# Four-layer block on one core: the token mix moved to VectorE, and token chunks 2 and 3 handled as one chunk of 1024 columns between the value stage and the step sizes

## The reference, cut to what matters

```
x = layernorm(x + attention(x))            # channel attention, 16 heads of 8
x = layernorm(x + ffn(x))                  # the change is in this layer and the next
x = layernorm(x + ssm(x))
x = layernorm(x + mlp(x))                  # 128 -> 512 -> 512 -> 512 -> 128

ffn:  x_prev = x shifted by one token (zero ahead of the first)
      xr = mu_r*x + (1-mu_r)*x_prev ;  xk = mu_k*x + (1-mu_k)*x_prev
      out = sigmoid(xr @ W_r) * (square(relu(xk @ W_k)) @ W_v)

ssm:  lifted = tanh(relu(x @ Wl1 + bl1) @ Wl2 + bl2)
      xt = relu(concat(x, lifted) @ Wf1 + bf1) @ Wf2 + bf2
      B = xt @ W2 + b2 ;  C = xt @ W3 + b3 ;  delta = softplus(xt @ W1 + b1)
      h = exp(-celu(delta*A)) * h0 + xt * delta * B       # 16 states, no recurrence over tokens
      out = sum over states of C * h
```

## Time and profile before

| what | us |
|---|---|
| median of 3 runs (lowest to highest) | 257.53 (257.16 to 259.03) |
| the profiled execution | 257.19 |
| its span, first to last instruction | 255.1 |
| busy of PE, DVE, ACT, POOL in the span | 230.5, 203.0, 185.4, 122.8 |

### The profile page before, as it was taken

One profiled execution on the slowest core, in us unless ns is written; L12 is line 12 of the kernel. 1 busy time (PEld: TensorE's weight loads), 2 busy tenths in 40 slices (PEclk: granted clock), 3 DMA queues, 4 the chain that ended last, 5 costly groups with the idle time before them and its releaser, 6 DMA issues.

```text
span 255.1 us, 2677 instructions
## 1 busy us (share of the span) xinstructions
PE 230.5 (90%) x871; PEld 151.4 (59%) x871; DVE 203.0 (80%) x328; ACT 185.4 (73%) x255; POOL 122.8 (48%) x96
## 2 busy tenths in 40 slices
PE   6898899999999867999686999999999899999981
PEld 6888557545433234545233556578888678888860
DVE  4996892698377799997999989980599997996454
ACT  4787799989898699979998986369943743643433
POOL 3410000000046998899999983473344578054220
PEclk9999999999999955999997999999999999999996
DMA  5960000000000000000000000000000000110002
GB/s 137 377 260 1 1 3 0 0 0 0 0 0 0 0 5 1 3 0 0 1 1 0 0 0 3 0 0 0 0 0 3 0 0 3 42 41 0 1 0 82
DMA packets 4847, 6.16 MB, mean 24 GB/s; under 512 B 384, under 2 KB 2656, under 8 KB 4832
## 3 DMA queue, kind: packets, MB, share of 16 engines
q1 hardware_dynamic: 4832, 5.97, 6.9%
HBM read 4.92 MB, written 1.05 MB: 23 GB/s over the span
## 4 chain that ended last, share of the span: by engine, by line
PE 47%; DVE 22%; ACT 11%; POOL 10%; issue 6%; DMA 2%; SPq 0%; ACTq 0%; POOLq 0%; DVEq 0%
PE ps L1419 8%; PE ps L1420 8%; PE ps L1309 6%; PE ps L217 3%; PE ps L219 3%; PE ps L218 3%; POOL bs L420 3%; PE ps L1207 3%; DVE tr L1060 2%; DMA bx<-in_x_dram 2%; PE ps L1285 2%; POOL tr_f L412 2%; DVE xr L1057 2%; DVE tr L1057 2%; POOL bxt L399 1%
## 5 line engine op out<-in xcount | busy, mean ns | idle before, releaser
L733 ACT ACTIVATE bs<-ps,vec 128x512 f32<-128x512 f32 x48 | 31.7, 690 | 37.3 <-PE ps L1420 34.9
L1285 PE MATMUL ps<-tr,h0sel 96*128 96x512 f32 x64 | 26.5, 530 | 10.8 <-DVE bx L967 3.8
L389 POOL CAST tr<-bs 96x512 fp32r<-96x512 f32 x4 | 2.4, 607 | 59.2 <-ACT bs L632 59.0
L1285 PEld LDWEIGHTS ps<-tr,h0sel 96*128 96x128 f32 x64 | 12.7, 215 | 24.1 <-issue 11.8
L1419 PE MATMUL ps<-xr,wf 128*128 128x512 f32 x64 | 25.4, 396 | 0.0
L1420 PE MATMUL ps<-xr,wf 128*128 128x512 f32 x64 | 25.3, 396 | 0.0
L462 POOL TENSOR_TENSOR xr<-bs,xr 128x512 fp32r<-128x512 f32 x12 | 16.1, 1347 | 14.0 <-DVE xr L1057 14.0
L462 POOL TENSOR_TENSOR tr<-bs,tr 128x512 fp32r<-128x512 f32 x8 | 10.9, 1361 | 22.3 <-DVE tr L1057 22.3
L462 POOL TENSOR_TENSOR x1r<-bs,x1r 128x512 fp32r<-128x512 f32 x12 | 13.5, 1128 | 9.5 <-DVE x1r L1057 9.5
L1057 DVE CAST tr<-bs 128x512 fp32r<-128x512 f32 x16 | 7.4, 488 | 13.3 <-ACT bs L733 13.3
L1309 PE MATMUL ps<-bx,centre 128*128 128x512 f32 x28 | 16.5, 726 | 0.0
(11 more groups left out here) (228 smaller groups left out, 678.4 us busy)
## 6 DMA issues: line engine op xcount, KB each, us to landing
wf_raw<-in_w_mlp_dram SPq DMA_DIRECT2D x2, 1024.0 KB, 8.6
bx<-in_x_dram SPq DMA_DIRECT2D x4, 256.0 KB, 5.3
out_dram<-bdl SPq DMA_DIRECT2D x4, 256.0 KB, 2.3
wf_raw<-in_w_mlp_dram SPq DMA_DIRECT2D x1, 768.0 KB, 12.5
bdl<-in_w_ssm_dram SPq DMA_DIRECT2D x1, 448.0 KB, 7.9
wa<-in_w_attn_dram SPq DMA_DIRECT2D x1, 256.0 KB, 2.7
w0raw<-in_w_ffn_dram SPq DMA_DIRECT2D x1, 192.0 KB, 7.3
h0T<-in_state_dram SPq DMA_DIRECT2D x1, 48.0 KB, 5.4
```

The source lines that it names most:

```text
L733: a.activation(hbuf[k][:, o, :], ring(mbank(i, stage, k, o)), ACT.Gelu if stage else ACT.Silu, scale=vec[:, s + o:s + o + 1]).then_inc(m_a ...
L1285: last = m.matmul(ps[:, 2 * j + k, :], h0sel[:, group_states(e)[j], :], tr[0:96, 0, cs(2 * (e // NG) + k)], start=True, stop=True)
```

## The change

1. The token mix leaves PE and its weights. DVE writes x straight into `x1_f32` (`first_input`), takes x - x_prev (`token_step`), and makes both mixes by one scalar_tensor_tensor each (`token_mix`). PE then needs one plain fp32 matmul for the key and one for the receptance of a chunk. `w0f`, `w0`, `mu1` and what made them go; the split of x goes.
2. Chunks 2 and 3 become one instruction of 1024 columns over two PSUM banks: on ACT from the key's Relu to `c_copy`, on DVE in `transformed`, `bounded`, `step_size`, `c_times_b`, `weighted`. The square of the second norm is merged for chunks 0 and 1 as well. `gate` and `second_input` stay single.
3. All four queues are reordered around it.

```diff
+            def first_input(c):
+                dve.wait_ge(y1_rs, c + 1)
+                v.tensor_tensor(shifted(0, c, 2), ps[:, 4 + c, :], bs2[:, cs(c)], ALU.mult).then_inc(x1_ok, 1)
+            def token_step(c):
+                dve.wait_ge(x1_ok, c + 1)
+                v.tensor_tensor(bx2[:, cs(c)], shifted(0, c, 2), shifted(0, c, 1), ALU.subtract).then_inc(step_ok, 1)
+            def token_mix(c, mu, dst):
+                dve.wait_ge(step_ok, c + 1)
+                v.scalar_tensor_tensor(dst, bx2[:, cs(c)], vec[:, mu:mu + 1], shifted(0, c, 1), ALU.mult,
+                                       ALU.add).then_inc(mixed, 1)
+            def mixes(c):
+                token_mix(c, MU_K, bx1[:, cs(c)])
+                token_mix(c, MU_R, shifted(1, c, 2))
```

```diff
             gate(0)
+            gate(1)
+            state_weights(11, 12)
+            gate(2)
+            gate(3)
+            state_weights(12, 14)
+            second_input(0)
+            second_input(1)
+            fill_low(5)
+            second_input(2)
             fill_low(6)
             fill_low(7)
...
             second_input(3)
...
             transformed(0)
             transformed(1)
+            fill_low(8)
             bounded(0)
+            fill_low(9)
             bounded(1)
+            state_weights(14, NS)
+            step_size(0)
             c_times_b(0)
-            step_size(0)
             step_size(1)
+            fill_low(10)
             c_times_b(1)
-            weighted(0)
             dve.wait_ge(a_ok, 2)
             dve.wait_ge(d_ps, 2)
-            state_v(0)
+            state_v(0, range(1))
+            weighted(0)
+            state_v(0, range(1, GN))
+            transformed(2, 2)
+            state_v(1)
             weighted(1)
-            transformed(2)
-            transformed(3)
-            state_v(1)
-            c_times_b(2)
-            c_times_b(3)
+            c_times_b(2, 2)
+            bounded(2, 2)
+            weighted(2, 2)
             dve.wait_ge(low_mm, 1)
             v.tensor_reduce(low_any[:, :], ps[:, FLAG_BANK, 0:NLOW], AX.X, ALU.add).then_inc(low_flag, 1)
-            bounded(2)
-            weighted(2)
-            weighted(3)
-            bounded(3)
             state_v(2)
             state_p(0)
+            step_size(2, 2)
             state_v(3)
-            step_size(2)
-            step_size(3)
             state_p(1)
```

ScalarE's new order (the second argument is the count of chunks):

```diff
             act.preload_act_table(ACT.Tanh)
+            receptance(0)
+            key_relu(0)
+            key_relu(1)
+            key_square(0)
+            receptance(1)
+            key_square(1)
             low_magnitude(0)
+            key_relu(2, 2)
+            key_square(2, 2)
+            receptance(2, 2)
+            square(y2_mm, y2_sq, 0, 2)
+            act.preload_act_table_set(LN_EXP)
+            rstd_of(y2_var, y2_ln, y2_rs, 0)
+            rstd_of(y2_var, y2_ln, y2_rs, 1)
+            square(y2_mm, y2_sq, 2, 2)
             fill_high(2 * FILL, 2 * FILL + 1)
...
             layer1(0)
+            rstd_of(y2_var, y2_ln, y2_rs, 2, 2)
             layer1(1)
             act.preload_act_table(ACT.Tanh)
             layer2(0)
+            layer2(1)
+            low_magnitude(1)
+            fill_high(2 * FILL + 1, 2 * FILL + 2)
+            layer1(2, 2)
+            fusion(0)
+            fusion(1)
             low_magnitude(2)
+            layer2(2, 2)
             act.preload_act_table_set(LN_EXP)
...
             log_exp(0)
+            fill_high(2 * FILL + 2, 2 * FILL + 3)
             log_ln(0)
             log_exp(1)
+            c_copy(0)
             log_ln(1)
             c_copy(1)
             act.wait_ge(a_ok, 2)
+            fusion(2, 2)
             state_t(0)
             state_t(1)
+            c_copy(2, 2)
+            low_magnitude(3)
             state_t(2)
             state_da(0)
             log_exp(2, 2)
+            log_ln(2, 2)
             state_t(3)
             state_da(1)
```

More of the change, by code:

```diff
@@ L422, in _ @@
             c_parts(0)
+            c_parts(1)
             pool.wait_ge(a_ok, 2)
@@ L557, in _ @@
                 rstd_of(y1_var, y1_ln, y1_rs, c)
[L559 to L566, removed]
-            def layer1(c):
-                act.wait_ge(l1_mm, c + 1)
-                a.activation(bs1[:, cs(c)], ps[:, 4 + c, :], ACT.Relu, bias=vec[:, BL1:BL1 + 1]).then_inc(l1_ok, 1)
@@ L573, in layer2, with receptance @@
-            def layer2(c):
-                act.wait_ge(l2_mm, c + 1)
-                a.activation(bs3[:, cs(c)], ps[:, c, :], ACT.Tanh, bias=vec[:, BL2:BL2 + 1]).then_inc(l2_ok, 1)
-            def fusion(c):
-                act.wait_ge(f1_mm, c + 1)
-                a.activation(bs1[:, cs(c)], ps[:, 4 + c, :], ACT.Relu, bias=vec[:, BF1:BF1 + 1]).then_inc(f1_ok, 1)
+            def receptance(c, count=1):
+                act.wait_ge(rec_mm, c + count)
+                act.wait_ge(y1_var, c + count)
+                a.activation(span(bs1, c, count), ps[:, c:c + count, :], ACT.Tanh, scale=0.5).then_inc(th_ok, count)
@@ new lines, in key_relu, with key_square, layer1 @@
+            def key_relu(c, count=1):
+                act.wait_ge(key_mm, c + count)
+                a.activation(span(bs2, c, count), ps[:, 4 + c:4 + c + count, :], ACT.Relu).then_inc(relu_ok, count)
+            def key_square(c, count=1):
+                s = slice(c * CH, (c + count) * CH)
+                act.wait_ge(relu_ok, c + count)
+                a.activation(bs3[:, s], bs2[:, s], ACT.Square).then_inc(k2_ok, count)
+            def layer1(c, count=1):
+                act.wait_ge(l1_mm, c + count)
+                a.activation(span(bs1, c, count), ps[:, 4 + c:4 + c + count, :], ACT.Relu,
+                             bias=vec[:, BL1:BL1 + 1]).then_inc(l1_ok, count)
@@ new lines, in layer2, with fusion @@
+            def layer2(c, count=1):
+                act.wait_ge(l2_mm, c + count)
+                a.activation(span(bs3, c, count), ps[:, c:c + count, :], ACT.Tanh,
+                             bias=vec[:, BL2:BL2 + 1]).then_inc(l2_ok, count)
+            def fusion(c, count=1):
+                act.wait_ge(f1_mm, c + count)
+                a.activation(span(bs1, c, count), ps[:, 4 + c:4 + c + count, :], ACT.Relu,
+                             bias=vec[:, BF1:BF1 + 1]).then_inc(f1_ok, count)
@@ L943, in c_times_b @@
-            def c_times_b(c):
-                dve.wait_ge(c_full, c + 1)
-                v.scalar_tensor_tensor(products[:, cs(c)], ps[96:128, c, :], vec[96:128, B23:B23 + 1],
-                                       bs3[0:32, cs(c)], ALU.add, ALU.mult).then_inc(bc_ok, 1)
-            def weighted(c):
-                dve.wait_ge(bc_mm, c + 1)
-                v.tensor_tensor(bxt[:, cs(c)], bxt[:, cs(c)], ps[:, c, :], ALU.mult).then_inc(w_ok, 1)
-            def state_v(e):
-                for j, n in enumerate(group_states(e)):
+            second_input(3)
@@ L956, in state_v @@
+            def state_v(e, group=range(GN)):
+                for j in group:
+                    n = group_states(e)[j]
                     if not v_on_pool(e, j):
```

223 lines of the change are left out of this document (96 added, 127 removed).

## The result

The changed kernel takes 261.33 us (median of 20 runs, 258.97 to 263.58); the kernel before, run beside it, takes 258.55 us (20 runs). The ratio is 1.0098, with a 95% interval of 1.0064 to 1.0133: slower by 2.5 us on 257.5. The two medians alone would give 1.0108; the ratio leaves out five of the 20 changed executions, those more than 1.5% above the fastest, all at a mean granted clock of 0.945 or less. The forecast was 258.9, which is 1.7 us over the profiled execution of before. The direction and the range (255.2 to 262.2) were right, the size was too small: the median lies above the range of the forecast itself (256.9 to 260.5) and within the whole one only because that has room for the rivals.

What follows compares the result with a forecast made beforehand. The prediction took queue order to decide from 54 to 89, then a DVE-bound scan. `state_v(2)` moves +1.7 us (+1.9 at first `transformed`, +0.8, -2.3, +1.3): 257.19 + 1.7 = 258.9, own range 256.9 to 260.5, whole range 255.2 to 262.2.

Steps and rivals of the forecast that it cites:

- What bounds the kernel: PE binds from 34.8 to 47.2, queue order decides from 54 to 89, DVE's own work sets the scan after.
- Part 1: Token mix to gates: gate 3 ends at 51.4 on PE, 2.5 us won.
- Part 2: Second norm to fusion: all 2.5 us lost and 2.6 more at second input; first `transformed` at 69.0, +1.9 us.
- Part 3: Step sizes to the scan: `state_v(2)` starts at 91.8 against 90.0 by the same bookkeeping, +1.7 us after rounding.
- bookkeeping: Calls dated in queue order by when engine and last input are free; said good to some 0.3 us.
- From `state_v(2)` on, all is shifted by a constant: Sign of being right: the scan starts late and everything after `state_v(2)` moves by the same amount.
- The merges win 1.7 us: Joining chunks 2 and 3: eleven ACT merges win 0.9 us, six DVE merges 0.8 us.
- The gates' lead kept: Faster rival, 12%: the gates' 2.5 us or the merges' 1.7 are kept; 254.7 us for the gates' lead.
- The clock earlier: Slower rival, 20%: half clock comes ahead of the scan; 261.7 us from 85 on, about 264.5 from 62 on.
- The scan swallowing the delay: No-change rival, 13%: the scan absorbs the delay or half of it, as DVE waited 1.75 us there; 257.5 us.

Runs made afterwards that it cites:

- e5: Changed kernel with its token mix kept, few pairs, and all queues from token mix to scan reordered from the dates; 253.67 us, ratio 0.9832 to before.
- e3: Changed kernel with one pair taken apart: Ln and Exp of the second norm for chunks 2 and 3; 258.44 us, ratio 1.0023 to before.
- e4: e3 with DVE's fills 6 and 7 moved behind the second input of chunk 3; 258.89 us, ratio 1.0045 to before.
- e7: Changed kernel in its own order, with all fifteen pairs taken apart where they stood; 255.45 us, ratio 0.992 to before.
- e11: e1 with only the change's seven late pairs put in, each where chunk 3's single instruction stood; 263.35 us, ratio 1.0186 to before.
- e1: Kernel before with only the change's token mix on DVE, old order of all queues, nothing paired; 257.63 us, ratio 1.0006 to before.
- e12: e5's order varied, with pairs where both inputs should be there; all queues differ and some e5 pairs are apart; 254.44 us, ratio 0.9836 to before.
- e6: Second hand-made order with the token mix on DVE: transformed 0 ahead of fusion 1, other places for fills; 255.6 us, ratio 0.9909 to before.
- e9: Changed kernel with only its seven late pairs (fusion to step_size) taken apart, the eight early ones kept; 259.01 us, ratio 1.0037 to before.
- e10: e7 with the token mix put back into PE's weights; 260.31 us, ratio 1.0067 to before.

## Why the prediction was right, and where it was off

- *What bounds the kernel*: right. The order of the queues sets the time; e5, with the changed kernel's arithmetic, is 2.7% faster than it.
- *Part 1, gate 3 at 51.4*: 51.8. The step that was mis-sized is "A token mix or step reads two SBUF operands of 512 columns: 0.69": the eight mixes of L898 took 0.75, the steps 0.69. The prediction had 0.75 as its upper bound and put it at 1 us "to a stage with slack"; eight mixes at 0.06 more are 0.5 us. The last mix ended at 42.73 (42.3), 0.4 us of it reached gate 3, and none was won back.
- *Part 2, the lead is lost at the paired normaliser*: right in mechanism and dates. Exp ends at 58.18 + 1.06 = 59.2 (58.7), DVE idles 2.81 (2.8), the second input 3 ends at 64.1 (63.7), the first `transformed` comes at 69.48 (69.0). e3 shows the cause: 1.9 us come back with this one pair apart.
- *Part 3*: right. `state_t(0)` 78.22 (77.9), `c_copy` 85.89 after 3.41 us idle (85.35 after 3.3), `weighted` 91.38 after 1.67 (90.6 after 1.7). `state_v(2)` came at 92.59 for 91.8: +2.84 on before's trace where the forecast had +1.7. Of the 1.1 us between them 0.4 is the mix's price, 0.25 the bookkeeping's own error on before (90.0 for 89.75), and the last 0.4 gathered in small steps between `state_t(0)` and `weighted`, in part because the last `b_times_c` ran 0.46 us longer at the lower clock than at the full one.
- *From `state_v(2)` on, all is shifted by a constant*: true of POOL's second `v_sum` (+2.56), not of the last add of the scan (+4.17), which comes behind the additional stretch at the lower clock. That the stretch costs 1.3 us of an execution is read from e3 against e4. By the mean clocks of the timed executions more time at the lower clock is some 0.6 us of the 2.5; the prediction had no such term in its forecast. What decides when such a stretch comes stays open.
- *The merges win 1.7 us*: the prices are right (ACT over two banks 1.11 and 1.12 for the 1.12 taken, DVE 1.27 to 1.29 for 1.27), but the win is not there. (On DVE five instructions were merged, not six, which makes 0.7 us of the 0.8.) Taken apart again, the fifteen pairs give 4.6 us (e7). The prediction priced the waits ahead of some pairs (the normaliser's, `fusion`, `c_copy`, `weighted`) and still booked a gain for the merges; it never priced the same order without pairs, which e7 shows to be the better kernel. The Trainium skill, "Perfetto Trace Analysis", section "Optimizing Scalar/DVE Operations", says that breaking up instructions may bring work sooner where ScalarE and VectorE aren't saturated but leave other engines waiting; e7 and e11 agree, with 4.6 us each.
- *Rivals.* The gates' lead kept (12%): not in the change, but in e7, where it is 2.1 us under before. The clock earlier (20%): by its own sign, 0.50 ahead of `state_ch(0)`, it came true, at a smaller price: the fall at 90.2 caught the last `b_times_c`, 0.46 us and not 2.8. That the median of 261.33 lies next to this rival's 261.7 is chance, for most of its loss comes from the pairs. In e11 the fall at 90.0 cost more, and in e1's profile there was one at 50. The scan swallowing the delay (13%): no; DVE's wait at the same place grew from 1.75 to 2.15 us. It does swallow an earlier start, in e12.

Four kernels beat both: e5 and e12, at ratios 0.9832 and 0.9836, and e6 and e7, at 0.9909 and 0.992.

## What to carry to other kernels

Before two chunks are joined into one instruction, compare when their inputs arrive: the join moves the first chunk to the second's date and its reader to the end of both, and 0.1 us of saved instruction doesn't pay for 1.8 us of waiting. In e12, with pairs only where both inputs should be there, there was no loss against e5, though the other differences of the two orders aren't told apart from it. A lead won in one stage is worth nothing until the order behind it is made to use it. The dates of all queues, written down from one trace's durations, told the times of the seven reorderings (e5, e6, e7, e9, e10, e11 and e12) to within 2.1 us. That found the better orders, but it is no fine tool: e7, e11 and e12 lie outside the ranges that were expected of them, and a difference of 1.6 us (e12 against e5) was beyond it.

## What was not expected of the hardware

- A `scalar_tensor_tensor` with a per-partition scalar from a vector took 0.75 us for 512 fp32 columns from SBUF (L898), where that with a constant (L931) took 0.69.
- The same idle time of TensorE is followed by half clock in one execution and not in another: 1.51 us ahead of 49.5 in e1 (0.50 from 50 to 53.4) and in e11 (1.00), 2.21 us in e3 (0.50 from 125.7 to 129.2) and 2.23 us in e4 (1.00). The Trainium skill, "TensorE: Matmul & The Clock Gate", part "The HAM clock gate", says that idleness brings the throttle back; e1 and e3 agree in direction, e11 and e4 show that these idle times alone don't decide it.
- One kernel's time varies with the mean granted clock of the execution: the changed kernel took 258.97 to 259.93 us in the four runs at 0.963, and 262.7 to 263.6 in those at 0.938 or 0.939. A difference of 1% between two single executions says little.
